# The causal mask under the decay of a ViT/mLSTM tower: mask and identity as fp32r operands in place of bfloat16

## What is computed

```
q = headwise(x_act, Wq); k = headwise(x_act, Wk); v = headwise(x_mlstm, Wv)
ig = (if_in @ W_ig + b_ig);  fg = (if_in @ W_fg + b_fg)
log_f = log_sigmoid(fg)
lfc = cumsum(log_f)                          # with a zero in front
lfm = where(causal mask, lfc - lfc^T, -inf)  # <- the mask
logD = lfm + ig^T
mD = max(logD, axis=-1)
Dmat = exp(logD - mD)
C = (q k^T) * DH ** -0.5 * Dmat
h = (C / (max(|sum C|, exp(-mD)) + 1e-6)) v
```

## Time and profile before

| | us |
|---|---|
| median of 3 runs | 728.7 |
| lowest, highest | 727.11, 731.2 |
| profiled execution | 731.04 |
| its span, from first to last instruction | 729.3 |
| TensorE busy (PE) | 651.3 |
| VectorE busy (DVE) | 471.1 |
| ScalarE busy (ACT) | 390.4 |

### The profile page before, as it was taken

The page is one execution under the profiler, slowest core; times in us unless marked ns, Lnnn a source line. Parts: engine busy times, 40 slices in busy tenths (PEclk is TensorE's granted clock), DMA queues, the critical chain, the costliest instruction groups (busy, mean ns, idle before and its releaser), DMA issues.

```text
span 729.3 us, 11752 instructions
## 1 busy us (share of the span) xinstructions
PE 651.3 (89%) x4013; PEld 546.4 (75%) x4013; DVE 471.1 (65%) x1529; ACT 390.4 (54%) x856; POOL 229.1 (31%) x249
## 2 busy tenths in 40 slices
PE   5799889999999999999999878858899999999992
PEld 3777768878878878878878857736678888888782
DVE  0543776876876876876876854556576767777670
ACT  0338638529529529529529518304366666666550
POOL 3000110143143143143143133145326666422541
PEclk9699899999999999999999977977999999999997
DMA  8239110020020020020010010026599999989860
GB/s 300 78 104 362 50 50 1 19 84 18 18 84 19 18 84 19 18 84 18 19 35 19 18 33 16 18 58 241 161 409 383 383 373 380 369 294 388 296 237 15
DMA packets 46260, 101.69 MB, mean 139 GB/s; under 512 B 10951, under 2 KB 32245, under 8 KB 41328
## 3 DMA queue, kind: packets, MB, share of 16 engines
q1 hardware_dynamic: 35184, 89.07, 33.9%
q0 software_dynamic: 9488, 8.52, 4.5%
q10 hardware_dynamic: 1520, 3.23, 1.3%
HBM read 80.17 MB, written 23.32 MB: 142 GB/s over the span
## 4 chain that ended last, share of the span: by engine, by line
PE 69%; DVE 14%; ACT 6%; issue 4%; POOL 3%; DMA 3%; SPq 0%; DVEq 0%; POOLq 0%
PE bank L1154 14%; PE bank L1922 14%; PE bank L1941 8%; PE bank L1277 5%; PE bank L1122 5%; PE bank L1256 3%; DVE stats_h L859 3%; PE bank L1180 2%; PE bank L1218 2%; POOL rstd_h L421 2%; PE bank L1930 2%; PE bank L1249 2%; PE bank L1266 2%; DVE h L902 1%; DMA bg<-b_zone_dram 1%
## 5 line engine op out<-in xcount | busy, mean ns | idle before, releaser
L421 POOL TENSOR_TENSOR rstd_h<-var_h,minus_half 76x4 f32<-76x4 f32 x32 | 32.3, 1010 | 227.0 <-DVE var_h L873 227.0
L1122 PE MATMUL bank<-patch,lin_w 128*128 128x288 f32 x192 | 52.7, 429 | 10.0 <-DMA col_t<-cols 7.8
L1922 PE MATMUL bank<-w_hi,x_hi 128*128 128x512 f32 x148 | 56.5, 463 | 3.2 <-DVE x_lo L1824 2.9
L1741 POOL DMA_INDIRECT out<-rows,bg x32 | 37.7, 1180 | 68.4 <-DVE rows L1812 61.4
L468 ACT ACTIVATE att_t<-bank 128x304 f32<-128x304 f32 x16 | 6.8, 424 | 92.9 <-PE bank L1277 92.2
L1122 PEld LDWEIGHTS bank<-patch,lin_w 128*128 128x128 f32 x192 | 37.3, 200 | 22.3 <-POOL v L398 7.8
L777 DVE SCALAR_TENSOR_TENSOR y<-xm,conv_t,y 128x296 f32<-128x296 f32 (+2 forms) x96 | 43.7, 511 | 10.2 <-ACT xm L468 10.2
L1922 PE MATMUL bank<-w_lo,x_hi 128*128 128x512 f32 x148 | 46.3, 394 | 0.0
L1922 PE MATMUL bank<-w_hi,x_lo 128*128 128x512 f32 x148 | 46.1, 393 | 0.0
L1848 DVE TENSOR_TENSOR act_e<-silu_e,bank 128x512 f32<-128x512 f32 x37 | 25.4, 687 | 29.4 <-PE bank L1922 29.4
L1818 DVE TENSOR_TENSOR w_lo<-wts,w_hi 128x1024 fp32r<-128x1024 f32 x36 | 43.1, 1218 | 0.6 <-ACT w_hi L1870 0.5
(11 more groups left out here) (249 smaller groups left out, 1793.4 us busy)
## 6 DMA issues: line engine op xcount, KB each, us to landing
wts<-w_exp SPq DMA_DIRECT2D x18, 1024.0 KB, 9.9
x_act<-w_exp SPq DMA_DIRECT2D x10, 1024.0 KB
silu_z<-w_exp SPq DMA_DIRECT2D x9, 1024.0 KB, 9.6
wts_down<-w_exp SPq DMA_DIRECT2D x18, 512.0 KB, 8.0
patch<-patches SPq DMA_DIRECT2D x8, 864.0 KB, 6.6
down_w<-w_exp SPq DMA_DIRECT2D x10, 512.0 KB, 8.3
lin_w<-w_exp SPq DMA_DIRECT2D x9, 512.0 KB, 9.1
b_zone_dram<-act_t SPq DMA_DIRECT2D x1, 4160.0 KB, 28.0
```

The source lines that it names most:

```text
L421: pool.tensor_tensor(rstd_h[:, j, :], var_h[:, j, :], minus_half[:], ALU.pow).then_inc(s_rstdh, 1)
L1122: last = pe.matmul(fb[c][:, 0:GS * N], lin_w[:, k, c * 128:(c + 1) * 128], patch[:, k, :], start=(k == 0), stop=(k == KF - 1))
L1741: pool.indirect_dma_start(out, bass.IndirectOffsetOnAxis(ap=rows_at, axis=0), rows[:, k % 4, :], None, bounds_check=T - 1, oob_is_err=Fals ...
L1922: last = pe.matmul(banks[2 + 2 * e + u][:, :], x[:, e, c * SLOT:(c + 1) * SLOT], w[:, e, u, c * I:(c + 1) * I], start=(n == 0), stop=(n == ...
```

## The change

`mask_bf` and `ident_bf` are gone. A new tile `mask_r`, fp32r, holds the mask; for the identity the product takes the top left 76x76 of `ident_r`. The two GpSimd instructions are taken out and `CONSTS` falls by two; VectorE makes `mask_r` in `centre_values`, in one instruction ahead of the copy to `pick`. Of each decay product, the values and the PSUM region are the same. The two small tiles took as many bytes in a partition as the new one does.

```
-        mask_bf = sb("mask_bf", [R, R], bf16)
-        ident_bf = sb("ident_bf", [R, R], bf16)
+        mask_r = sb("mask_r", [R, R], f32r)
...
-        CONSTS = 13 + TS + 1
+        CONSTS = 11 + TS + 1
...
-            pool.tensor_scalar(mask_bf[:], tri[:], -1.0, -MASKED, ALU.add, ALU.mult).then_inc(s_const, 1)
-            pool.tensor_copy(ident_bf[:], ident[0:R, 0:R]).then_inc(s_const, 1)
...
                 dve.wait_ge(s_const, CONSTS)
+                dve.tensor_scalar(mask_r[:], tri[:], -1.0, -MASKED, ALU.add, ALU.mult)
                 dve.tensor_copy(pick[:], pick_raw).then_inc(s_prep, 1)
...
-                pe.matmul(ab[j][0:R, 0:GT], ident_bf[:], mask_bf[:].unsqueeze(1).broadcast_to([R, NH, R]),
+                pe.matmul(ab[j][0:R, 0:GT], ident_r[0:R, 0:R], mask_r[:].unsqueeze(1).broadcast_to([R, NH, R]),
                           start=True, stop=False)
```

## The result

The changed kernel is slower: a median of 737.4 us (733.5 to 739.6) against 731.2 us for the kernel before (727.1 to 732.0), seven runs each; the ratio is 1.0085, 95% interval 1.0064 to 1.0107, or 6.2 us. The forecast was 1.1 us more, 729.8 us, and called it the same; the time lies above its range, which ended at 732.7. It is 7.6 us above the forecast: 5.1 us because the change cost 6.2 and not 1.1 us, and 2.5 us because the three runs of before that the forecast started from had a median of 728.7, where seven have 731.2. In all that follows, a ratio is against the kernel before, run beside it on the same chip, and executions over 1.5% above the fastest of their kernel are left out of it: one each of e6, e12 and e13.

A forecast was written before the change was run, and what follows sets the result against it. TensorE was taken to bound the kernel; longer mask loads and streams added 0.89 us at full clock and 0.24 at half, together +1.1 on the 728.7 us median: 729.8 us, counted as the same, range 727.0 to 732.7.

The forecast's parts named there:

- What bounds the kernel: TensorE, busy for 89% of the span and 69% of the chain; 28 of 32 mask matmuls lie on the chain.
- The drains: Gaps behind and ahead of the mask go with array rows in use, 48 against 76 or 128, and stay.
- Rival A: Gaps around the mask belong to the type, so all-fp32r decays hide weight loads: 5.0 us less, 723.7 us; chance 7%.
- rival B: The fp32r mask, read with step 0, streams at plain float32 pace: 733.1 or 740.4 us; chance 5%.
- The load term: The mask's unhidden weight load grows from 111 to 139 ns, +28 ns at full clock; +59 ns at half.
- the streaming term: The mask's stream and fixed tail grow from 211 to 220 ns, +9 ns at full clock; 0 at half.
- The sum of 1.1: Microseconds added on TensorE: 24 masks at 37 ns (0.89 us) plus 4 at 59 ns (0.24 us).
- The preparation: At the start, GpSimd's some 0.5 us gain hides behind a DMA; VectorE's added instruction hides in idle time: 0 counts.
- The step that failed: On TensorE's chain, 24 masks count at full clock, 4 at half; waiting engines and expert weights simply move with it.
- The half-clock share: 4 of the 28 mask matmuls on the chain, those of group 7, run at 1.2 GHz, +59 ns each.

The follow-up runs named there:

- e6: Kernel before with one bfloat16 matmul of 96 columns added ahead of each mask product, lengthening the decays; ratio 1.0076.
- e12: e6 with one matmul of 304 columns left out of each group's last but one up projection; ratio 1.0011.
- e13: Kernel before with one matmul of 304 columns left out of each group's last but one up projection, decays untouched; ratio 1.0069.
- e5: Kernel before with the running maxima padded from 48 to 72 rows of zeros, mask still bfloat16; ratio 0.9926, 725.1 us.
- e2: Changed kernel's preparation (VectorE makes mask and identity, two constants fewer to wait for) with the bfloat16 product of the kernel before; ratio 1.0010.
- e7b: Kernel before with one fp32r matmul of 304 columns added in each group's last but one up projection, decays untouched; ratio 1.0111.
- e3: Changed kernel (fp32r mask) with the running maxima padded from 48 to 72 rows of zeros; ratio 0.9982.
- e9b: Changed kernel with one matmul of 304 columns left out of each group's last but one up projection, fp32r decays untouched; ratio 1.0057.
- e4: Changed kernel with every fp32r mask product issued twice, the second overwriting the first; ratio 1.0237.
- e11: e5 with the transpose ahead of the decays widened from 16 to 72 rows too; ratio 0.9947.

## Why the prediction was wrong

**What bounds the kernel** held: the mask's piece grew on the chain by what its record grew, in groups 1 to 7.

**The drains** held, and the runs add the proof that the trace before could not give: with 72 rows beside 76 they go, and with alternating types they stay away (e5). Rival A, that the type drains, is out: mask to follower is 0.29 us in the changed kernel, not 0.14. So is rival B, half the pace: one record, 362 ns.

**The load term** was 28 ns and measured 32 (143 against 111), **the streaming term** 9 and measured 8 (362 - 143 against 322 - 111); at the half clock 59 became 62 to 63. The sum of 1.1 is 1.2 us. The section on the weight load in the Trainium skill ("TensorE: Matmul & The Clock Gate", "LDWEIGHTS") knows no difference by type; the rows decide against it.

**The preparation** held: VectorE's new instruction takes 0.18 us and waits for TensorE afterwards as before, GpSimd's gain hides behind the DMA, and e2 measures 1.0010 with an interval that contains 1.

**The step that failed** is the one behind the sum: "24 of the 28 count at the full clock and 4 at the half", with "what ScalarE, VectorE and the expert weights wait for starts from TensorE's results and moves with it". It took the granted clock of the profile before as given, and a delay on the chain as a shift that changes nothing else. The runs show that the clock is part of the answer: the direct cost is 1.2 of the 6.2 us, and the 5 us left are laid to falls at the decays, of which the profiled execution has 6.0 us. Two causes stand behind them. The step is shown: 0.14 us in either direction, in bfloat16, with untouched decays, costs 0.7 to 1.1% (e13, e7b), and taking the step back takes the loss away (e12 against e6). That it works by a drift against fixed moments (D) fits the places of the falls, but it is argued, and its forecast for e3 missed. The fp32r mask itself is the second: padded, at the same step, it is slower and has falls where bfloat16 has none (e3 against e5: the two intervals touch, 0.9952 and 0.9954, but on the same chip all nine executions of e5 took 726.2 us or less and ten of e3's twelve took more); without padding, e9b against e12 says the same, but narrowly and with another start. How the 5 us divide between them isn't settled, since they don't add: fp32r at nearly the old step makes about 4 (e9b less 0.2 direct), the step in bfloat16 about 4 to 7 (e6 less its 1.2 direct, e13 plus the 1.0 it saves, e7b less its 1.0). Nor is it settled what in the fp32r mask does it; that more streaming helps is refuted only for a lengthened step (e4, e6).

The half-clock share in the failed step is also no fixed 4 of 28: in the changed kernel's profile a fifth was there, the last of group 5. The prediction had no rival for this, and its range rested on the spread of the kernel before, whose clock had been steady where it counts.

## What to carry to other kernels

Where TensorE sets the length of a loop, count the falls of the granted clock and their places in the loop before pricing a small edit; here an edit of 0.3% of the loop made the kernel 0.7 to 1.1% slower, whether it added work (e7b) or left some out (e13). Compare several executions, and read the price of the edit from undisturbed turns of the loop. Look for gaps between matmuls on different rows of the array: padding 48 rows to 72, next to 76, was worth 0.5 to 0.7% here in bfloat16 (e11, e5), and that step of 53.9 us brought no falls at the decays either. In fp32r it won 1.0% against the changed kernel (0.9982 against 1.0085), and the falls stayed.

## What the runs showed of the hardware

- A weight load of 76 columns that nothing hides took 143 ns in fp32r and 111 ns in bfloat16 at 2.4 GHz, 201 and 139 ns at 1.2 GHz.
- Between matmuls of 48 and of 76 rows the next weight load did not lie beside the matmul, which made the mask's piece 0.12 us longer (0.25 against 0.13) and that of its four followers 0.15 us (0.39 against 0.24); between 72 and 76 rows it did, with the type changing (e5) or not (e3).
- The granted clock fell to 0.50 in stretches in which TensorE was busy for all of the time, 3.40 of 3.40 us, and had been ahead of them, 3.50 of 3.50 us. From group 1's decays to 20 us behind group 6's, in all profiled executions, every fall began between 1.6 and 4.2 us behind the first mask of a group, that is in the decays or in the up projection right behind them.
